# Cross-attention with group norm on one core: ScalarE's shift ahead of r's copy, the weights on the context tiles' queue, and the last seven steps written out in another order

## What is computed

```
q = Wq y + bq ;  k = Wk y + bk ;  v = Wv x + bv            # per batch, 128 x 1024
scores = q k^T / sqrt(128)          # per head, 16 x 16: over the 1024 columns
attn   = softmax(scores)
o      = Wo (attn v) + bo + x
out    = (o - mean(o)) * rsqrt(var(o) + 1e-5) * gn_w + gn_b   # mean, var over the whole batch
```

## Time and profile before

| | |
|---|---|
| median of 3 runs | 166.63 us (166.38 to 167.06) |
| the profiled execution's own time | 166.47 us |
| its span in the trace | 164.6 us |
| busy in the span | PE 94%, DVE 91%, ACT 83%, PEld 74%, POOL 60% |
| TensorE's granted clock | full in every stretch until 160 us |
| DMA | 50.84 MB, mean 309 GB/s |

### The profile page before, as it was taken

How to read it: one execution, slowest core, us unless ns; L and a number is a source line. 1 busy time by engine, 2 the same in 40 slices (tenths; PEclk the granted TensorE clock), 3 DMA queues, 4 the chain that set the end, 5 groups by cost and what they waited for, 6 DMA issues and landing times. The chain is left out here.

```text
span 164.6 us, 3752 instructions
## 1 busy us (share of the span) xinstructions
PE 154.2 (94%) x932; PEld 121.0 (74%) x932; DVE 149.5 (91%) x686; ACT 137.2 (83%) x354; POOL 98.0 (60%) x162
## 2 busy tenths in 40 slices
PE   7998999999999999999999999999999999998820
PEld 7896887777777788887777777888777777785500
DVE  1788999999999999999999999999999999987861
ACT  3685499999999999999999999999999999767351
POOL 3039267776666676667766666766777666541120
PEclk9999999999999999999999999999999999999995
DMA  5999859999999999998999999999999977631136
GB/s 188 403 407 412 313 196 330 324 338 296 350 342 348 346 357 396 345 336 272 380 377 354 336 344 351 358 334 339 329 374 338 377 308 263 255 127 59 75 127 255
DMA packets 14277, 50.84 MB, mean 309 GB/s; under 512 B 1712, under 2 KB 1712, under 8 KB 14256
## 3 DMA queue, kind: packets, MB, share of 16 engines
q1 hardware_dynamic: 13824, 50.08, 83.3%
q10 hardware_dynamic: 432, 0.53, 0.9%
HBM read 33.82 MB, written 16.78 MB: 307 GB/s over the span
## 5 line engine op out<-in xcount | busy, mean ns | idle before, releaser
L751 PE MATMUL o_ps<-x_sb,m_sb 128*128 128x512 f32 x124 | 61.1, 612 | 0.7 <-ACT out_sb L404 0.7
L751 PE MATMUL g_ps<-hl_sb 128*128 128x258 f32 x256 | 47.0, 308 | 0.0
L484 DVE TENSOR_TENSOR hl_sb<-y_sb,hl_sb 128x512 fp32r<-128x512 f32 x64 | 43.7, 687 | 0.0
L574 DVE BATCH_NORM_STATS2 bn<-o_ps 128x6 f32<-128x512 f32 x62 | 40.3, 685 | 1.4 <-PE o_ps L751 1.4
L325 ACT CAST hl_sb<-y_sb 128x512 fp32r<-128x512 f32 x64 | 39.2, 618 | 1.9 <-DMA y_sb<-in_ctx_dram 1.9
L404 ACT ACTIVATE out_sb<-o_ps,shift,gain 128x1024 f32<-128x1024 f32 x31 | 37.4, 1206 | 2.6
L252 POOL TENSOR_TENSOR lsuma<-hl_sb 128x256 f32<-128x256 f32 x30 | 21.9, 729 | 25.9 <-DVE hl_sb L484 25.9
L751 PEld LDWEIGHTS g_ps<-hl_sb 128*128 128x128 f32 x256 | 35.5, 194 | 0.2 <-DVE hl_sb L484 0.2
L263 POOL TENSOR_TENSOR lsumb<-hl_sb 128x256 f32<-128x256 f32 x30 | 21.9, 729 | 17.5 <-DVE hl_sb L484 17.5
L751 PEld LDWEIGHTS o_ps<-x_sb,m_sb 128*128 128x128 f32 x124 | 21.0, 191 | 14.7 <-issue 14.7
L274 POOL TENSOR_TENSOR lsum<-lsuma,lsumb 128x256 f32<-128x256 f32 x30 | 22.3, 743 | 4.2 <-issue 0.4
(11 more groups left out here) (76 smaller groups left out, 288.9 us busy)
## 6 DMA issues: line engine op xcount, KB each, us to landing
y_sb<-in_ctx_dram SPq DMA_DIRECT2D x32, 512.0 KB, 6.3
x_sb<-in_x_dram SPq DMA_DIRECT2D x32, 512.0 KB, 7.1
out_dram<-out_sb SPq DMA_DIRECT2D x31, 512.0 KB, 6.3
w_in<-in_weights_dram ACTq DMA_DIRECT2D x1, 256.0 KB, 5.4
out_dram<-out_sb ACTq DMA_DIRECT2D x1, 256.0 KB, 2.6
out_dram<-out_sb SPq DMA_DIRECT2D x1, 256.0 KB, 2.8
cols<-in_columns_dram ACTq DMA_DIRECT2D x1, 3.0 KB, 3.4
```

The costliest lines, as they stand in the source:

```text
L484: nc.vector.tensor_tensor(hl_sb[:, b % SLOTS, chunks, C:2 * C], y_sb[:, b % SLOTS, chunks, :], hl_sb[:, b % SLOTS, chunks, 0:C].bitcast(F3 ...
L574: nc.vector.bn_stats(bn[:, b % 2, half, :], o_half(b, half)).then_inc(bn_done, 1)
L751: return nc.tensor.matmul(dst, lhsT, rhs, start=start, stop=stop, **more)
```

## The change

The weights' transfer moves from ACT's queue to SP's, between the first and the second context tile. In ACT's loop `write_shift(t - 5)` moves ahead of `copy_r(t - 3)`. The loops of PE, DVE, ACT and POOL end two steps earlier, and those two steps and the drain are written out in another order, with some waits added for batches from 26 (`LATE`) on, which order instructions of one engine or guard a buffer. All instructions of before are still there; none is added.

```diff
+        LATE = LAST - 5
...
-            for b in range(SLOTS):
+            load_y(0)
+            sp.dma_start(w_in[:, :, :].rearrange("p w c -> p (w c)"), weights).then_inc(w_loaded, 16)
+            for b in range(1, SLOTS):
                 load_y(b)
...
             act.dma_start(cols[:, :], columns).then_inc(c_loaded, 16)
-            act.dma_start(w_in[:, :, :].rearrange("p w c -> p (w c)"), weights).then_inc(w_loaded, 16)
...
-            for t in range(4, B):
+            for t in range(4, LAST - 1):
                 exponential(t - 3)
                 round_half(t, 1)
                 normalise(t - 3)
                 write_gain(t - 5)
                 scale_bk(t - 2)
+                write_shift(t - 5)
                 copy_r(t - 3)
-                write_shift(t - 5)
                 output(t - 5)
                 copy_cross(t - 1)
                 round_half(t + 1, 0)
...
             def deviation(b):
                 if not live(b):
                     return
+                if b >= LATE:
+                    dve.wait_ge(cp_ready, b + 1)
                 dve.wait_ge(mv_ready, b + 1)
...
             def input_product(b, half):
...
-                    if b >= LAST - 2:
+                    if b >= LATE:
                         pe.wait_ge(m_copied, b + 1)
                         pe.wait_ge(x_in[b % SLOTS], loads(b))
```

More of the change, by code:

```diff
@@ L721, in _ @@
             statistics_of(b - 1, 0)
+            shift_by_pivot(b - 2)
             deviation(b - 2)
```

153 lines of the change are left out of this document (128 added, 25 removed).

## The result

The change makes the kernel a little slower. Its median is 167.24 us (166.51 to 171.15 in 20 runs) against 166.56 us (166.19 to 167.10 in 20 runs) for the kernel before on the same chip; the ratio is 1.0036 with a 95% interval of 1.0022 to 1.0049. The profiled execution took 166.81 us, with a span of 164.9 us. The forecast was 165.3 us with a range of 164.4 to 166.6: wrong in sign, and outside its range.

What follows compares the result with a forecast made beforehand. Late steps were taken to hang on ACT's chain, the ramp on the columns and first context tile. Gains of 0.7 + 0 + 0.6 = 1.3 us gave a median of 165.3 us, range 164.4 to 166.6.

Steps and rivals of the forecast that it cites:

- Part 1: ACT's loop: shift ahead of the copy of r brings late steps from 4.520 to 4.484 us, gain 0.7 us.
- Part 2: Ramp: weights on SP's queue end DVE's 0.64 us wait for them; gain 0 to 0.05 us, counted as 0.
- at worst it lands at 6.4: Ramp: tile 1, behind the weights, lands by 6.4 us instead of about 5.8, and is needed at 6.45.
- I take 0: Ramp: the price of tile 1 standing behind the weights in SP's queue was put at 0 us.
- it buys nothing: Ramp: ending DVE's wait for the weights gains nothing, as the rest of batch 1 waits for ACT's rounding until 7.09.
- Part 3: Last seven steps: the new order gives 0.7 us less 0.1 for costs, net 0.6, bounds -0.3 to 1.1.
- rival A: Only the loop gains, as DVE's idle before batch 28's statistics delays batch 30's scores; 165.9 us, 15 in 100.

Runs made afterwards that it cites:

- e15: e9 with the weights ahead of the small columns on ScalarE's queue; 170.81 us, ratio 1.0270 to the kernel before.
- e1: The changed kernel with the weights back on ScalarE's (ACT's) queue; 166.24 us, ratio 0.9984 to the kernel before.
- e2: The kernel before with only the weights moved to SP's queue behind tile 0; 168.02 us, ratio 1.0081 to the kernel before.
- e4: e1 with the variance of batch 26 back ahead of the Gram sum on DVE; 166.08 us, ratio 0.9970 to the kernel before.
- e5: The kernel before with the shift moved, plus two already met waits on DVE's Gram sum and column sum from batch 2 on; 166.57 us.
- e12: e7 with only the added waits of deviation and variance put off until batch 29; 165.50 us, ratio 0.9946 to the kernel before.
- e9: e7 with the added waits only from batch 29 on instead of 26; 165.02 us, ratio 0.9913 to the kernel before.
- e7: The kernel before with the shift moved in the whole loop (to t = 31), then the changed kernel's drain order and all added waits; 166.08 us.
- e14: e7 with all added waits except those of deviation and variance put off until batch 29; 165.51 us, ratio 0.9942 to the kernel before.
- e17: e9 with deviation's added wait, for cp, in every step from batch 2 on; 166.16 us, ratio 0.9975 to the kernel before.
- e18: e9 with variance's added wait, for rstd, in every step from batch 2 on; 167.26 us, ratio 1.0039 to the kernel before.
- e10: e7 with query, scores and minimum of batch 30 back in the order of before on PE, DVE and ACT; 166.51 us, ratio 0.9999.
- e6: The kernel before with the shift moved and the weights on SP's queue behind tile 1; 165.97 us, ratio 0.9966 to the kernel before.
- e8: e7 with the Gram sum and column sum of batch 31 ahead of the reciprocal of batch 30 on DVE; 166.38 us, ratio 0.9980.
- e16: e9 with the weights ahead of tile 0 on SP's queue; 166.48 us, ratio 0.9982 to the kernel before.

## Why the prediction was wrong

**Part 1** was right: late steps of 4.48 to 4.49 us against a forecast of 4.484, 0.55 us in the median and 0.62 in the loop's term for a forecast of 0.7. The output starts 0.45 us nearer to the copy (131.33 - 130.88 is 0.45, not 0.44). The slack of `r`'s copy held.

**Part 2** failed at "at worst it lands at 6.4". The sum of bytes over rate is right (e15 shows it: tile 1 at 6.00 us with the weights ahead of it in another queue), but it takes the queue to run at the rate of the earlier trace rows without a hitch. In SP's queue, behind the weights, tile 1 landed at 7.26 to 7.62 us in three kernels. That cost 0.9 us (after against e1) to 1.5 us (e2) where I had put 0. The trace of before did not show such packets. "I take 0" with no bound above it was the mistake: the bound was a transfer at full rate. The reading of the ramp was off as well. In before's profiled execution the Gram product of batch 0 held minimum 2, and by the 12.92 us above tile 1's rounding could have started at 6.91 instead of 6.45 for nothing (19.83 - 12.92). In an execution like e1's it costs from 6.45 on (19.37 - 12.92). And "it buys nothing" for the weights does not hold in most executions: in nine of the 15 minimum 2 hangs on the weights, and in e1, e4, e5 and e12 they make it 0.2 to 0.4 us later than the Gram product alone would. That the ramp hangs on the columns and on tile 0 left out these ties.

**Part 3** failed at "the other waits added from batch 26 on are for things done a step before, and cost nothing". Put off until batch 29 (e9 against e7), they give 1.06 us in the medians and 0.71 in the terms behind the ramp. Two mechanisms carry it, shown apart by e12 and e14, and the first one also by e17 and e18. A second wait on a short instruction of a full engine makes it start later, though that wait was met long ago: 0.07 to 0.08 us on `deviation`, whose operand the aggregate has just written, and 0.05 on `variance`. That puts 0.016 and 0.06 us on each step. And a single delay of about 0.2 us stands at a fixed count of DVE's instructions and waits (number 575), so that added waits move what it meets. The prediction charged a handover for the `deviation` of step 31 alone.

The rest of Part 3 was about right. Without those waits, the stretch from minimum 27 to input product 31 is 21.24 us (forecast 21.2). Output 28 starts 6.97 us behind input product 28 (7.58 before), 0.61 us earlier, for a forecast of 0.8. Two small terms were missed. Behind input product 31 the new order costs 0.16 us in every kernel that has it: `shift_by_pivot` and a wait for `cp` stand ahead of the last statistics and the last deviation, but which of them costs it was not tried. And the order of `variance(b - 5)` in step 30 costs 0.10 us through POOL.

So of the forecast sum of 1.3 us, 0.98 is in e9's profiled execution (160.45 - 159.47), whose ramp was as slow as before's, and 1.5 in its median. The forecast of gain was near the mark for a kernel that had neither the new place of the weights nor the early waits. Of rival A's reason, the late scores of batch 30, e10 shows that it was not the cause.

## What to carry to other kernels

A wait that is already met is not free on an engine that has no gaps: it cost 0.016 to 0.06 us a step here, so put it only where the order needs it, and count it when an order is changed. Where a transfer has 0.05 us of slack, its forecast needs a bound for a queue that stumbles and not only bytes over rate; leave such a transfer alone, or put the new one behind it (e6). Read a ramp in more than one execution, since its binding tie can change from one to the next. Judge a bundle of changes part by part: here one part gave 0.55 us, one took 0.9 to 1.5, and the third turned from a loss into a gain with one constant.

## What the runs showed of the hardware

- A semaphore wait that was met long before delays a dependent short instruction on VectorE: 0.10 to 0.11 us behind its operand's end instead of 0.03 (e17, e7 against e9). The Trainium skill, VectorE: DVE Perf Modes, section "The DRAIN you can't avoid", says that a semaphore after each of eight copies costs nothing extra. That is one semaphore for each instruction; for a second one these runs show a price.
- Single delays of about 0.2 us stand at fixed places of an engine's instruction stream. DVE's are 384 instruction records apart in e5 (numbers 191 and 575, steps of 4.71 us twice); e17 has the first of the two places, and after, e1, e4, e7, e8, e10 and e12 have the second. The other kernels show no such delay at these numbers; in them number 575 comes right behind long instructions. The late start of POOL's sum in the 4.77 us step, 0.42 to 0.43 us idle, stands at one place in all 20 kernels. What causes them was not tried.
- A 128x1 power on GpSimd took 1.06 instead of 0.55 us when it began 0.02 us behind a VectorE instruction with two SBUF operands (e4 against e1). The other way round, 128x1 operations of VectorE with SBUF operands took 0.37 and 0.33 instead of 0.16 and 0.21 us when they began during a sum on GpSimd, and ended with it (the 4.77 us step).
- TensorE's granted clock fell to 0.50 for over 6 us after a ramp in which PE had been busy 1.78 of 4.5 us (e15), and for over 10 us in one execution after 3.16 of 4.5 us (e16); with 3.88 of 5 us busy it stayed at 1.00 in the changed kernel's profiled execution.
- Single 4 KB packets took 1.0 to 1.5 us at 4.1 to 4.6 us of the span in the three kernels with the weights ahead of tile 1 in SP's queue, against at most 0.37 us in the 17 others at that time.
- The same two products at the start took TensorE 1.22 us in seven profiled executions and 0.70 to 0.82 in eight, with a granted clock of 1.00 in the rows of before and of e1. Their ramps end on different ties. Why they differ is open.
